# A graph layer with sorted gathers: loops written out, gathers paced by TensorE, row numbers copied once a block

## Chip, cores and metric

The kernel runs on one core of a Trainium2 chip. The metric is the time of one execution on the device in microseconds (us). TensorE multiplies matrices, VectorE and ScalarE work elementwise, GpSimd issues the gathers here, SyncE issues the plain transfers.

## What is computed

x has 50000 nodes of 128 features. 25000 edges carry 128 features each and name a node `src`; the sum of a node's edges is joined to the node's normalised features.

```python
h = jnp.maximum(_layernorm(x, axis=-1), 0.0)
agg = jax.ops.segment_sum(edge_attr, src, num_segments=50000)
z = jnp.concatenate([h, agg], axis=-1)            # 256 wide
z = jax.nn.silu(z @ W1 + b1)                      # W1 256 x 256
z = z @ W2 + b2                                   # W2 256 x 128
z = layernorm(z) * ln_gamma + ln_beta
out = x + (z + h)
```

## The kernel before

The work has two phases. In the **column phase** the 25000 edge numbers lie in 196 columns of 128. For each column VectorE makes one-hot matrices (`hot_tile`, `hot_slot`), TensorE counts with them (L601, L608) and fills a table (L613), and ScalarE reads ranks (L513, `rank_of`); three columns of 28 are VectorE's. At its end VectorE has turned the table into `slot_edge`: for each of 392 tiles of nodes, which edge stands in which of 128 slots (`slot_tables`, the first three blocks' part first).

In the **block phase** the nodes are taken in NB = 49 blocks of 1024 (8 tiles of 128, in two halves c = 0, 1 of four). GpSimd gathers each tile's edge rows from memory into `G[b % 3]` by an indirect DMA (L471). The row numbers are a column of `gather_rows`, which GpSimd copies from `slot_edge` just before (L459, `name_row`). The order of a gather's steps is: wait until `agg_done` says that block b-3 has left the buffer, copy the next tile's row numbers, wait for `row_named`, issue. Nothing else holds a gather back.

TensorE's `step(b)` is, for c = 0 and then 1: transpose four tiles of h (`turn_h`, L636: in c = 0 the second half of b, in c = 1 the first half of b+1), sum the gathered edges of that half by one-hots (`sum_edges`, L643, waits for `gathered`), layer 1 of half c (`layer1`, L654 to L659, two column groups m = 0, 1, each ends with `pre_done`), and layer 2 of the half before (`layer2`, L667 and L671, ends with `y_done`). ScalarE normalises x (L534), copies the high parts of `za` to `hi` (L541, L543), applies silu (L549) and squares y (L556). VectorE subtracts to get the low parts (L911, `split_low`, the first thing in its step), builds the one-hots HOT (L902), adds x and beta (L894), h (L919), takes statistics and reciprocal roots (`powers`), and scales the result (L927, L937). SyncE loads X four blocks ahead and stores R two blocks behind. The order on each engine is written out by hand; semaphores join the engines.

Both phases are loops. `run_columns` writes 28 columns out, then loops over turns of 28. `run_blocks` writes out the first `head` blocks (2 on ScalarE and SyncE, 3 on TensorE and GpSimd, 5 on VectorE), then loops over turns of 6 blocks, and writes out what is left, for TensorE blocks 39 to 48. In a loop, semaphore values and addresses are registers (`Turn`), and each wait on a register is an instruction of its own. A second copy of the whole gather code, from the table `spill`, runs instead when a tile has more edges than slots; it does not here, and stands ahead of the main copy. The loops' branches are at L285 (blocks) and L296 (columns).

## Time and profile before

| what | value |
|---|---|
| median of 3 runs | 835.01 us (830.93 to 836.53) |
| the profiled execution, its own time | 833.45 us |
| its span, first to last instruction | 831.8 us |
| busy share: TensorE, VectorE, GpSimd, ScalarE | 88%, 88%, 74%, 70% |
| mean granted TensorE clock | 0.957 |
| mean transfer rate | 79 GB/s |

The profiled time is the span and 1.65 us around it. A busy share is an average over both phases. The column phase ends near 125 us, where GpSimd begins its first copy of row numbers; everything after it is the block phase. A wait in the profile is named by what ended it; "issue" means that the profile shows no event that the engine waited for, and "remote" that it knows no instruction for the event.

### The profile page before, as it was taken

To read this page: it belongs to the slowest core of one execution; us is meant where nothing else is said; L and a number is where in the kernel's file an instruction comes from. 1 tells how busy PE (TensorE), PEld (TensorE's weight loads), DVE (VectorE), ACT (ScalarE), POOL (GpSimd) and SP (SyncE) were. 2 spreads that over 40 slices of the span, in tenths; PEclk is the share of its full clock that TensorE was granted. 3 is DMA by queue.
4 is the path that set the end of the run, shared out by engine and by line. 5 is a ranking of instruction groups with operands and counts; after the bars stand their busy time and mean duration, and the time that the engine had idled before them with its cause. 6 is when DMAs were issued, how large, how long until landed. Compare 5 with 4: busy or idle time off the path is not lost.

```text
span 831.8 us, 19347 instructions
## 1 busy us (share of the span) xinstructions
PE 734.6 (88%) x4567; PEld 602.0 (72%) x4616; DVE 734.0 (88%) x2494; ACT 585.6 (70%) x1927; POOL 617.9 (74%) x831
## 2 busy tenths in 40 slices
PE   4999973899899678998999899989988998989990
PEld 2455542788787657887888788878877887878880
DVE  6999994799996748998999899989888999997995
ACT  4999972687675636787687777868567877776861
POOL 4500006899888887999999989999898899898920
PEclk9999995999999988999999999999999999999996
DMA  5000000123232222332323223232323233231211
GB/s 185 2 0 0 0 0 18 47 71 111 84 122 73 71 73 69 120 121 70 119 76 115 94 93 121 87 103 93 98 73 118 83 107 122 72 102 60 69 58 46
DMA packets 28138, 65.49 MB, mean 79 GB/s; under 512 B 8379, under 2 KB 9934, under 8 KB 28070
## 3 DMA queue, kind: packets, MB, share of 16 engines
q1 hardware_dynamic: 15526, 51.90, 17.5%
q0 software_dynamic: 12544, 12.93, 6.9%
q14 instruction: 54, 0.44, 0.2%
q8 instruction: 14, 0.23, 0.1%
HBM read 51.98 MB, written 25.60 MB: 93 GB/s over the span
## 4 chain that ended last, share of the span: by engine, by line
POOL 35%; issue 26%; PE 25%; DVE 5%; ACT 3%; another core or an unknown queue 2%; DMA 2%; POOLq 1%; DVEq 0%; ACTq 0%; SPq 0%
POOL G L471 22%; POOL gather_rows L459 13%; PE y L671 4%; PE y L613 3%; PE za L643 3%; PE pre L654 2%; PE pre L655 2%; PE pre L659 2%; PE za L608 2%; PE pre L608 2%; PE pre L601 2%; PE za L636 1%; PE za L601 1%; DMA G<-in_edge_attr_dram,gather_rows 1%
## 5 line engine op out<-in xcount | busy, mean ns | idle before, releaser
L471 POOL DMA_INDIRECT G<-in_edge_attr_dram,gather_rows x392 | 450.1, 1148 | 69.1 <-POOL gather_rows L459 41.2
L459 POOL COPY gather_rows<-slot_edge 128x1 uint32 (+1 forms) x392 | 145.9, 372 | 98.4 <-DVE slot_edge L883 91.7
L671 PE MATMUL y<-w2c,S 128*128 128x128 f32 x1568 | 194.2, 276 | 6.5 <-issue 3.2
L671 PEld LDWEIGHTS y<-w2c,S 128*128 128x128 f32 x1568 | 192.9, 193 | 7.8 <-issue 5.3
L911 DVE TENSOR_TENSOR lo<-za,hi 128x1024 fp32r<-128x1024 f32 x98 | 119.7, 1221 | 72.5 <-ACT hi L543 37.8
L534 ACT ACTIVATE H<-X,shift,rstd 128x128 f32<-128x128 f32 x392 | 162.3, 505 | 22.7 <-DVE shift L793 22.7
L654 PE MATMUL pre<-hi,w1h 128*128 128x512 f32 x392 | 168.0, 429 | 0.7 <-issue 0.7
L655 PE MATMUL pre<-hi,w1l 128*128 128x512 f32 x392 | 158.8, 405 | 0.3
L541 ACT CAST hi<-za 128x512 fp32r<-128x512 f32 x98 | 57.5, 587 | 118.0 <-remote 55.0
L549 ACT ACTIVATE S<-pre,b1c 128x512 f32<-128x512 f32 x196 | 125.7, 693 | 9.2 <-remote 4.9
L659 PE MATMUL pre<-lo,w1h 128*128 128x512 f32 x392 | 125.9, 402 | 0.7 <-issue 0.7
L643 PE MATMUL za<-HOT,G 128*128 128x128 f32 x784 | 110.5, 286 | 17.8 <-DMA G<-in_edge_attr_dram,gather_rows 16.6
L643 PEld LDWEIGHTS za<-HOT,G 128*128 128x128 f32 x784 | 100.1, 200 | 20.8 <-DMA G<-in_edge_attr_dram,gather_rows 19.3
L738 DVE BATCH_NORM_STATS2 stat<-X 128x6 f32<-128x128 f32 x392 | 108.6, 283 | 0.0
L556 ACT ACTIVATE junk_sq<-y 128x128 bf16<-128x128 f32 x392 | 103.5, 287 | 3.5 <-PE y L671 3.5
L927 DVE SCALAR_TENSOR_TENSOR T<-y,rstd,gammas 128x128 f32<-128x128 f32 x392 | 105.6, 341 | 0.0
L543 ACT CAST hi<-za 128x512 fp32r<-128x512 f32 x98 | 57.6, 588 | 58.6 <-PE za L643 41.8
L636 PE MATMUL za<-ident,H 128*128 128x128 f32 x392 | 61.7, 281 | 37.3 <-ACT H L534 17.5
L659 PEld LDWEIGHTS pre<-lo,w1h 128*128 128x128 f32 x392 | 75.5, 193 | 19.3 <-issue 0.8
L654 PEld LDWEIGHTS pre<-hi,w1h 128*128 128x128 f32 x392 | 77.3, 197 | 15.0 <-issue 0.9
L655 PEld LDWEIGHTS pre<-hi,w1l 128*128 128x128 f32 x392 | 76.9, 196 | 15.4 <-issue 1.4
L556 ACT ACTIVATION_READ_ACCUMULATOR junk_sq<-y 128x1 f32 x392 | 85.5, 218 | 0.0
(123 smaller groups left out, 1042.2 us busy)
## 6 DMA issues: line engine op xcount, KB each, us to landing
X<-in_x_dram SPq DMA_DIRECT2D x48, 512.0 KB
out_dram<-R SPq DMA_DIRECT2D x48, 512.0 KB
G<-in_edge_attr_dram,gather_rows POOLq DMA_INDIRECT x392
X<-in_x_dram SPq DMA_DIRECT2D x1, 424.0 KB
out_dram<-R SPq DMA_DIRECT2D x2, 212.0 KB
w1f<-in_L_gnn_W_dram SPq DMA_DIRECT2D x1, 256.0 KB, 3.5
w2f<-in_L_gnn_W_dram SPq DMA_DIRECT2D x1, 128.0 KB, 2.7
srci<-in_src_dram SPq DMA_DIRECT2D x1, 97.2 KB
```

The costliest lines, as they stand in the source:

```text
L459: nc.gpsimd.tensor_copy(gather_rows[b.xj][:, t:t + 1], slot_edge[:, bass.ds(b.number(TILES, t), 1)]).then_inc(row_named, 1)
L471: nc.gpsimd.indirect_dma_start(G[b.j][:, t, :], None, source, bass.IndirectOffsetOnAxis(ap=gather_rows[b.xj][:, t:t + 1], axis=0), bounds_ ...
L534: done = nc.scalar.activation(H0[b.j][:, t, :], X[b.xj][:, t, :], ACT.Relu, bias=shift[b.j][:, t:t + 1], scale=rstd[b.j][:, t:t + 1])
L549: nc.scalar.activation(S[c][:, m, :], pre[m][:], ACT.Silu, bias=b1c[:, m:m + 1]).then_inc(silu_done, 1)
L556: done = nc.scalar.activation(junk_sq[:, p, c * HALF + t, :], y[2 * p + c][:, t * D:(t + 1) * D], ACT.Square, scale=float(D) ** -0.5, accu ...
L643: done = nc.tensor.matmul(za[:, 1, t * P:(t + 1) * P], G[b.j][:, c * HALF + t, :], HOT[b.j][:, c * HALF + t, :], start=True, stop=True)
L654: nc.tensor.matmul(pre[m][:], w1h[:, k, cols], hi[c][:, k, :], start=(k == 0), stop=False)
L655: nc.tensor.matmul(pre[m][:], w1l[:, k, cols], hi[c][:, k, :], start=False, stop=False)
L659: done = nc.tensor.matmul(pre[m][:], w1h[:, k, cols], lo[c][:, k, :], start=False, stop=(k == 1))
L671: done = nc.tensor.matmul(place[:, t * D:(t + 1) * D], S[c][:, m, t * P:(t + 1) * P], w2c[:, m, :], start=False, stop=(t == HALF - 1 and m ...
L738: done = nc.vector.bn_stats(stats[b.ring(2)][:, t, :], X[b.xj][:, t, :])
L911: nc.vector.tensor_tensor(out=lo[c][:], in0=za[:], in1=hi[c][:].bitcast(F32), op=ALU.subtract).then_inc(lo_done, 1)
```

## The change

All loops over columns and blocks are written out, so that semaphore values and addresses are constants. GpSimd copies the eight row numbers of a block in one instruction (`name_rows`), half a block ahead. A gather's wait for the freed buffer is replaced by a wait for an event on TensorE (`pace`): the four gathers of half c of block b+2 wait for the sum of edges in half-step c of TensorE's step b, for the two `pre_done` of that half-step's layer 1, and for its layer 2. The first two blocks are not paced. The spill copy of the gather code stands behind the main one.

```diff
-TURN_BLOCKS = 6
...
-        def run_blocks(engine, step, head=HEAD):
-
-            turns = (NB - 1 - head - X_AHEAD) // TURN_BLOCKS
-            for n in range(head):
+        def run_blocks(step):
+
+            for n in range(NB):
                 step(Block(n))
-            with engine.Fori(0, turns) as i:
-                turn = Turn(engine, i)
-                for n in range(head, head + TURN_BLOCKS):
-                    step(Block(n, TURN_BLOCKS, turn))
-            for n in range(head + turns * TURN_BLOCKS, NB):
-                step(Block(n))
-
-        def run_columns(engine, step, lag):
-
-            for n in range(UNROLL):
-                step(Item(n))
-            with engine.Fori(0, TURNS - 1) as i:
-                turn = Turn(engine, i)
-                for n in range(UNROLL, 2 * UNROLL):
-                    step(Item(n, UNROLL, turn))
-            for n in range(EC, EC + lag):
+
+        def run_columns(step, lag):
+
+            for n in range(EC + lag):
                 step(Item(n))
...
-            def name_row(b, t):
-
-                if t == 0:
-                    at_least(pool, agg_done, b.half(0, 1, 2 - 2 * X_RING), apart=pool_passed)
-                    if b.is_number(FIRST_BLOCKS):
-                        pool.wait_ge(slots_ready, 2)
-                nc.gpsimd.tensor_copy(gather_rows[b.xj][:, t:t + 1],
-                                      slot_edge[:, bass.ds(b.number(TILES, t), 1)]).then_inc(row_named, 1)
-
-            def gather(b, c, source, limit):
-
-                at_least(pool, agg_done, b.half(0, 1, 2 - 2 * RING), apart=pool_passed)
+            def name_rows(b):
+
+                at_least(pool, agg_done, b.half(0, 1, 2 - 2 * X_RING))
+                if b.is_number(FIRST_BLOCKS):
+                    pool.wait_ge(slots_ready, 2)
+                nc.gpsimd.tensor_copy(gather_rows[b.xj][:],
+                                      slot_edge[:, bass.ds(b.number(TILES), TILES)]).then_inc(rows_named, 1)
+
+            def pace(b, c, k):
+
+                if k == 0:
+                    at_least(pool, agg_done, b.half(1, 1, c + 1))
+                elif k == 3:
+                    at_least(pool, y_done, b.half(c, 1))
+                else:
+                    at_least(pool, pre_done, b.half(c, 2, k))
+
+            def gather(b, c, source, limit, pacer=None):
+
                 for t in range(c * HALF, (c + 1) * HALF):
-                    if t + 1 < TILES:
-                        name_row(b, t + 1)
-                    elif b.plus(1).exists(NB):
-                        name_row(b.plus(1), 0)
-                    at_least(pool, row_named, b.number(TILES, t + 1), apart=pool_passed)
+                    if t == HALF and b.plus(1).exists(NB):
+                        name_rows(b.plus(1))
+                    if t == 0:
+                        at_least(pool, rows_named, b.number(1, 1))
+                    if pacer is not None:
+                        pace(pacer, c, t - c * HALF)
                     nc.gpsimd.indirect_dma_start(
...
-                            gather(b.plus(2), c, source, limit)
-
-                run_blocks(pool, step, head=3)
+                            gather(b.plus(2), c, source, limit, pacer=b)
+
+                run_blocks(step)
...
-            name_row(Block(0), 0)
+            name_rows(Block(0))
+            with pool.If(flag == 0):
+                gather_all(edge_attr, edges - 1)
             with pool.If(flag != 0):
                 gather_all(spill, NB * BLOCK - 1)
-            with pool.If(flag == 0):
-                gather_all(edge_attr, edges - 1)
```

On GpSimd, before, this is the entry of the block loop in the main copy of the gathers, from the first branch on; `row_named` counts the copies, and an ISA row is a register or semaphore instruction.

```order
L285 UNCONDITIONAL_BRANCH
L285 ISA
L459 ISA [waits agg_done]
L459 COPY gather_rows<-slot_edge 128x1
L471 DMA G<-in_edge_attr_dram,gather_rows 128x128 [waits row_named]
L459 ISA
L459 COPY gather_rows<-slot_edge 128x1
L471 DMA G<-in_edge_attr_dram,gather_rows 128x128 [waits row_named]
L459 ISA
```

On GpSimd, after, this is one block and the head of the next in the middle of the block phase; L417 is the copy and L438 the gather.

```order
L438 DMA G<-in_edge_attr_dram,gather_rows 128x128 [waits agg_done,rows_named]
L438 DMA G<-in_edge_attr_dram,gather_rows 128x128 [waits pre_done] x2
L438 DMA G<-in_edge_attr_dram,gather_rows 128x128 [waits y_done]
L417 COPY gather_rows<-slot_edge 128x8 [waits agg_done]
L438 DMA G<-in_edge_attr_dram,gather_rows 128x128 [waits agg_done]
L438 DMA G<-in_edge_attr_dram,gather_rows 128x128 [waits pre_done] x2
L438 DMA G<-in_edge_attr_dram,gather_rows 128x128 [waits y_done]
```

Eight pairs of copy and gather have become one copy and eight gathers, and every gather has a wait on TensorE that it did not have.

On VectorE, before, this is the end of the block loop's body, its branch, and what follows the loop; L911 is the first instruction of a step, so that it stands at the head of the body too.

```order
L919 TENSOR_TENSOR R<-H,R 128x512 [waits h0_done,xb_done]
L764 REGISTER_ALU
L791 SCALAR_TENSOR_TENSOR rstd<-guess_off,guess 128x16 [waits small]
L764 REGISTER_ALU
L793 SCALAR_TENSOR_TENSOR shift<-msum,rstd 128x8 [waits small]
L285 REGISTER_ALU
L285 COMPARE_AND_BRANCH
L911 TENSOR_TENSOR lo<-za,hi 128x1024 [waits pre_done,hi_done]
L902 TENSOR_TENSOR HOT<-iota_node,slot_node 128x512 [waits agg_done]
```

On VectorE, after, this is the same place between two steps (L886 was L919, L878 was L911).

```order
L886 TENSOR_TENSOR R<-H,R 128x512 [waits h0_done,xb_done]
L758 SCALAR_TENSOR_TENSOR rstd<-guess_off,guess 128x16 [waits small]
L760 SCALAR_TENSOR_TENSOR shift<-msum,rstd 128x8 [waits small]
L878 TENSOR_TENSOR lo<-za,hi 128x1024 [waits pre_done,hi_done]
L869 TENSOR_TENSOR HOT<-iota_node,slot_node 128x512 [waits agg_done]
```

The branch and the register instructions are gone; the order of the others is the same.

## Rows read from the trace of the kernel before

**Rows 1.** The page: TensorE and VectorE busy, and the chain by engine.

```profile
PE 734.6 (88%) x4567; PEld 602.0 (72%) x4616; DVE 734.0 (88%) x2494; ACT 585.6 (70%) x1927; POOL 617.9 (74%) x831
...
POOL 35%; issue 26%; PE 25%; DVE 5%; ACT 3%; another core or an unknown queue 2%; DMA 2%; POOLq 1%; DVEq 0%; ACTq 0%; SPq 0%
```

**Rows 2.** Timeline of TensorE at S(0), S(8), S(13), S(15), S(32), S(39), S(48): start, duration.

```profile
141.65 0.66 PE L636 MATMUL za<-ident,H 128*128 128x128 f32 x2 [2.02 <-DVE lo L911]
...
247.93 0.49 PE L636 MATMUL za<-ident,H 128*128 128x128 f32 x3
...
335.87 0.60 PE L636 MATMUL za<-ident,H 128*128 128x128 f32 x4
...
360.46 0.60 PE L636 MATMUL za<-ident,H 128*128 128x128 f32 x4
...
582.98 0.38 PE L636 MATMUL za<-ident,H 128*128 128x128 f32 x2
...
678.99 0.49 PE L636 MATMUL za<-ident,H 128*128 128x128 f32 x3
...
799.92 0.49 PE L636 MATMUL za<-ident,H 128*128 128x128 f32 x3
```

**Rows 3.** Windows: stretch and length, busy per engine (count), clock, DMA share, GB/s.

```profile
247.93:335.87 87.94, 70.63 (x407) 59.51 (x411) 62.06 (x214) 48.69 (x160) 75.07 (x105) 0.90 0.27 84
...
354.80:379.40 24.60, 24.46 (x165) 21.57 (x166) 24.50 (x86) 19.41 (x65) 22.29 (x29) 1.00 0.32 104
```

**Rows 4.** GpSimd's two groups on the page, and timeline rows beside VectorE's.

```profile
L471 POOL DMA_INDIRECT G<-in_edge_attr_dram,gather_rows x392 | 450.1, 1148 | 69.1 <-POOL gather_rows L459 41.2
L459 POOL COPY gather_rows<-slot_edge 128x1 uint32 (+1 forms) x392 | 145.9, 372 | 98.4 <-DVE slot_edge L883 91.7
...
134.95 1.03 POOL L471 DMA_INDIRECT G<-in_edge_attr_dram,gather_rows  x1 [0.16 <-POOL gather_rows L459]
...
157.58 0.68 DVE L894 TENSOR_TENSOR R<-X,betas 128x512 f32<-128x512 f32 x1
157.64 0.68 POOL L459 COPY gather_rows<-slot_edge 128x1 uint32<-128x1 uint32 x1
...
158.48 1.39 POOL L471 DMA_INDIRECT G<-in_edge_attr_dram,gather_rows  x1 [0.16 <-issue]
```

**Rows 5.** Waits from 678 to 800, then block 44's last gather and its sum.

```profile
PE za L643 <- DMA G<-in_edge_attr_dram,gather_rows: 6.1, 2, 4.1
...
742.00 1.30 POOL L471 DMA_INDIRECT G<-in_edge_attr_dram,gather_rows  x1 [0.16 <-POOL gather_rows L459]
...
742.79 0.28 SPq L332 DMA_DIRECT2D X<-in_x_dram  x1
...
749.51 1.86 PE L643 MATMUL za<-HOT,G 128*128 128x128 f32 x8 [4.09 <-DMA G<-in_edge_attr_dram,gather_rows]
```

**Rows 6.** Timeline at one of the turns of VectorE's loop.

```profile
392.44 1.23 DVE L911 TENSOR_TENSOR lo<-za,hi 128x1024 fp32r<-128x1024 f32 x1 [2.94 <-issue]
...
393.81 0.63 PE L636 MATMUL za<-ident,H 128*128 128x128 f32 x4 [2.45 <-DVE lo L911]
```

**Rows 7.** Waits (total, times, longest): ScalarE and TensorE 247 to 336, ScalarE 582 to 679.

```profile
ACT hi L541 <- remote: 26.8, 5, 9.5
...
PE y L671 <- issue: 3.2, 9, 0.5
...
ACT hi L541 <- remote: 12.1, 5, 4.3
```

**Rows 8.** Window in the column phase, columns as in rows 3.

```profile
59.00:74.00 15.00, 14.79 (x88) 8.23 (x87) 14.43 (x43) 14.72 (x53) 0.00 (x0) 1.00 0.00 0
```

**Rows 9.** Timeline of the first gathers, and TensorE's first sum.

```profile
128.12 0.20 POOL L459 COPY gather_rows<-slot_edge 128x1 uint32<-128x1 uint32 x1 [2.19 <-issue]
...
130.57 1.25 POOL L471 DMA_INDIRECT G<-in_edge_attr_dram,gather_rows  x1 [2.25 <-issue]
...
137.55 0.58 PE L643 MATMUL za<-HOT,G 128*128 128x128 f32 x1 [5.18 <-DMA G<-in_edge_attr_dram,gather_rows]
```

65 lines of the change are left out of this document (23 added, 42 removed).

## The prediction

> **What bounds the kernel now.** I read the page first, then the windows, then the timeline of TensorE, and last the timelines of the engines that TensorE waits for. The page says that TensorE and VectorE are each busy 88% of the span and that the chain that ended last gives most of its length to GpSimd and to "issue" [rows 1]. So no engine is simply full; one has to ask block by block who is late.
>
> The ruler for that is the first transpose of the second half of a block (L636), which opens block b's step on TensorE. Call its start S(b). S(0) is 141.65, S(8) 247.93, S(13) 335.87, S(15) 360.46, S(32) 582.98, S(39) 678.99, S(48) 799.92 [rows 2]. From S(13) to S(15) it takes 24.59 us for two blocks, 12.29 us a block. In that stretch TensorE is busy 24.46 of 24.60 us and VectorE 24.50, with a granted clock of 1.00, the level of 2.4 GHz [rows 3]: TensorE is full, VectorE nearly so, and GpSimd has 2.3 us to spare. Thus 12.29 us is the floor of a block for this arithmetic. 48 blocks at the floor are 590 us; S(48)-S(0) is 658.3, so **68.4 us are lost** in the block phase. By stretch, time less 12.29 a block: blocks 0 to 8: 106.3 - 98.3 = 8.0; 8 to 13: 87.9 - 61.5 = 26.5; 13 to 32: 247.1 - 233.5 = 13.6; 32 to 39: 96.0 - 86.0 = 10.0; 39 to 48: 120.9 - 110.6 = 10.3.
>
> Who takes them? A gather on GpSimd alone takes 1.03 us [rows 4], but their mean is 1.148 and that of the copy before each is 0.372, since VectorE's two-input instructions hold them up: beside x plus beta (L894) a copy took 0.68 and a gather 1.39 [rows 4]. With the 0.16 us between copy and gather a tile costs 1.148 + 0.372 + 0.16 = 1.68 us, a block 13.4 us: **more than the floor**. GpSimd never waits for another engine to speak of; it issues gathers without a pause and loses about 1.1 us a block on TensorE until TensorE waits for it, unless something else has held TensorE up before. Two of the stretches (0 to 8, 39 to 48) are of this kind: in the last, TensorE waits 6.1 us for gathered rows in two waits of up to 4.1, with what follows each [rows 5]. The stretch 13 to 32 is another kind. Three times VectorE's first instruction after its loop's branch (L911) starts some 3 us late with "issue" as the reason, and TensorE's next transposes wait on it: 2.94 and then 2.45 us at 392 to 394 [rows 6]; three such turns make most of the 13.6 us, 4.2 apiece with what is lost around them. The stretch 8 to 13 has one such turn and 22 us more whose cause I can't read: ScalarE waits 26.8 us in five waits for something "remote" (the trace names no releaser), and TensorE's granted clock was 0.90 in the mean, part of it at the lower level of 1.2 GHz [rows 3]. Blocks 32 to 39 have the same sign, 12.1 us of it [rows 7].
>
> **The change part by part.**
> (1) *One copy of row numbers per block.* GpSimd loses seven copies, 7 x 0.372 = 2.6 us a block; the 0.16 ahead of each gather I keep. What is left is 8 x (1.148 + 0.16) plus one copy of eight columns. No row shows that copy; the one-column copy runs 0.37 in the mean and 0.68 where it is held up, and twice that bounds it above, so 0.2 to 1.4, and I take 0.4, as eight numbers a partition are still few. 10.5 + 0.4 = 10.9 us a block, under 12.29 by 1.4 (by the bounds 1.6 to 0.4). GpSimd stops being the late one. Worth: 8.0 + 10.3 us in the stretches it rules, and its part of blocks 32 to 39.
> (2) *No block loops.* The three turns in 13 to 32 go, most of 13.6 us; one turn in 8 to 13 goes (4.2) and one in 32 to 39 (4). Registers that carried semaphore values go too; TensorE has no idle time for these in the floor stretch, so I cost them at nothing, hidden under matmuls.
> The Trainium skill (Runtime: NRT & Kernel Launch, Instruction fetch mechanics) says that each engine fetches its instructions in order ahead of use and that a taken branch out of the fetched pages stalls until the target is fetched; by that rule, the late L911 right behind VectorE's branch is a fetch, and it vanishes in straight code. The sum above goes by the rows alone.
> (3) *No column loops.* Before the blocks ScalarE is busy 14.72 of 15 us at ranks [rows 8], instruction behind instruction. A loop's branch leaves no idle time to recover: nothing, at most 2 us.
> (4) *The spill branch behind the main one, and the start.* GpSimd loses 2.19 and 2.25 us to "issue" around the first gathers, and TensorE waits 5.18 us for the first gathered rows [rows 9]. The second pause follows the branch that jumps over a whole copy of the gather code, which now stands behind. Bounds 0 to 4.4 us, plus 0.6 for the three copies that no longer stand between the first four gathers (3 x 0.35 = 1.1 us, less what the larger first copy takes). I take 3 us.
> (5) *The added waits.* Gather t of a half of block b+2 now waits for agg_done, pre_done twice and y_done of TensorE's half-step of block b. Behind a waiting gather GpSimd has only later gathers and the next block's copy queued. The last gather of a half is freed when that half-step ends and its rows are wanted two half-steps after that, by sum_edges one whole block later: 12.29 us, less 1.39 for the gather itself, 10.9 us to land. What landing takes: the first rows came 1.6 us after their fourth gather's end [rows 4, 9], and the longest that I found is block 44's, whose last gather ends at 743.30 and whose sum starts at 749.51, 6.2 us [rows 5], just as SyncE had issued a block's load. So 4.7 us remain in the worst row: I cost the waits at nothing. They are hidden by that slack; if it were gone, each us of excess would cost 1 us a block.
>
> **Sum.** Saved without dispute: 8.0 + 10.3 + 13.6 + 4.2 + 4 = 40.1, and 3 at the start: 43.1. In dispute: the 22.3 us left in blocks 8 to 13 and 6 us in 32 to 39, 28.3 together. That they are of the loops speaks that both lie inside them while the straight stretch 39 to 48 has nothing of the kind beside its gather waits; against it speaks that blocks 13 to 32 lie in loops too and are clean. I let two thirds go, 19. I keep 2 us lost in the first blocks, where VectorE also makes the slot tables. 43.1 + 19 - 2 = 60 us. The span becomes 831.8 - 60 = 772, the profiled time 833.45 - 60 = 773.5; the median of the runs (835.01) lies 1.6 above the profiled one, so **775 us**.
> Bounds: all 68.4 gone, 4.4 at the start and 2 in the columns make 75 us: 760. None of the disputed 28.3 and nothing at the start give 43.1 - 3 - 2 = 38 us: 797.
>
> **Rivals.**
> *The disputed stalls stay* (they are no loop's and no gather's): 794 to 797, worked out just now. Chance 0.17.
> *The floor falls too.* Seven fewer reads by GpSimd might speed VectorE, and all stalls go: 760 or less. But TensorE is full at 12.29, so VectorE's gain buys nothing. 0.07.
> *GpSimd meets VectorE more often.* Paced by TensorE, each gather falls on the same VectorE instruction in every block. If all eight were beside two-input ones, as the 1.39 row, a block would be 8 x (1.39 + 0.16) + 0.8 = 13.2 us, 0.9 over the floor, 48 x 0.9 = 44 us more: 818. Against: those instructions fill under half of VectorE's time and come in different half-steps. 0.04. The Trainium skill (SBUF — State Buffer, SBUF: two separate sides) states the rule behind it, that the port pair shared by GpSimd and VectorE is an exclusive lock that whoever comes first holds for the whole instruction; the 1.39 against 1.02 agrees.
> *Slower: straight code starves an engine.* Each turn's stall was 4.2 us, with "issue" and no event as its reason, as where instructions aren't at hand. The unrolled code has some two and a half times as many different instructions on TensorE. If that fails at one place in every block, 48 x 4.2 = 202 us are added; it outweighs the saving from 15 stalls on, one in three blocks. For it: in blocks 8 to 13 TensorE waited nine times with "issue" before layer-2 matmuls [rows 7]. Against it: blocks 39 to 48 are straight code on every engine and hold the floor in between two gather waits. 0.03, at about 850 or more.
> *The pacing doesn't pace, or delays nothing* is no case of its own: the time is as forecast.
>
> **How the numbers follow.** Forecast (two stretches freed, turns gone, part of the disputed gone; 760 to 790): 0.69. Range 760 to 797: it takes in forecast and the first rival, 0.86, less the edges. A measurement of this kernel can tell about 1% from no change. Faster by over 1%: 0.69 + 0.17 + 0.07 + 0.04 = 0.97, less 0.01 for the spread of the last (818); within 1%: 0.01; slower: 0.03.
>
> **What would show it.** Right: GpSimd's idle time before gathers is released by TensorE's sums and matmuls, S(b) advances by 12.29 us in nearly every block, no L911 starts 3 us late behind a branch, and no wait of TensorE for G is over 1 us after block 1. GpSimd's mean gather stays near 1.15. Wrong: TensorE waits for G again (port or landing), "issue" before TensorE or VectorE once in some blocks (delivery of instructions), or a block that takes over 12.6 us with TensorE full, which would say that my floor isn't one.

## The result and the profile after

The changed kernel takes 811.33 us in the median of four runs (809.54 to 812.34), the kernel before 834.88 beside it (830.93 to 836.53): a ratio of 0.972 [0.968, 0.976]. It is faster, by 23.5 us. The forecast was 775 us, in a range of 760 to 797. The sign is right, and less than half of the gain is there. The profiled run took 809.54 us with a span of 808.0. Here and below a median is of all runs, while a ratio and its interval leave out runs over 1.5% above the fastest of their kernel.

First, the page of the changed kernel: the engines, the chain by engine, and the groups that matter. L603 is the transposes (L636 before), L610 the sum of edges (L643), L508 and L510 ScalarE's two high copies (L541 and L543), L878 VectorE's low copy (L911), L438 the gather.

```profile
PE 723.1 (89%) x4567; PEld 591.0 (73%) x4616; DVE 730.6 (90%) x2494; ACT 581.6 (72%) x1927; POOL 502.9 (62%) x488
...
PE 63%; ACT 17%; DVE 8%; issue 7%; another core or an unknown queue 3%; DMA 1%; SPq 0%; POOL 0%; DVEq 0%; ACTq 0%; POOLq 0%
...
L438 POOL DMA_INDIRECT G<-in_edge_attr_dram,gather_rows x392 | 470.7, 1201 | 162.4 <-issue 105.7
...
L878 DVE TENSOR_TENSOR lo<-za,hi 128x1024 fp32r<-128x1024 f32 x98 | 119.7, 1222 | 51.3 <-ACT hi L510 47.1
...
L508 ACT CAST hi<-za 128x512 fp32r<-128x512 f32 x98 | 58.2, 594 | 90.8 <-PE za L603 63.5
L510 ACT CAST hi<-za 128x512 fp32r<-128x512 f32 x98 | 57.6, 587 | 79.5 <-remote 63.3
...
L610 PE MATMUL za<-HOT,G 128*128 128x128 f32 x784 | 105.5, 278 | 2.4 <-DMA G<-in_edge_attr_dram,gather_rows 2.4
...
L603 PE MATMUL za<-ident,H 128*128 128x128 f32 x392 | 62.7, 283 | 41.1 <-issue 23.9
```

Against [rows 1], GpSimd has left the chain (35% to 0%) and fell from 74 to 62% busy. TensorE waits for gathered rows 2.4 us in all. That is what the change is for, and it works. But TensorE now waits 41.1 us at its transposes, and ScalarE 79.5 us before its second high copy, mostly for "remote".

With the prediction's ruler, S(b):

```profile
137.29 1.09 PE L603 MATMUL za<-ident,H 128*128 128x128 f32 x4 [2.02 <-DVE lo L878]
...
158.09 0.60 PE L603 MATMUL za<-ident,H 128*128 128x128 f32 x4
...
776.21 0.60 PE L603 MATMUL za<-ident,H 128*128 128x128 f32 x4
```

S(0) is 137.29 (141.65 before, [rows 2]), S(1) 158.09, S(48) 776.21. The start gave 4.4 us. The block phase fell from 658.3 to 638.9 us, so that 638.9 - 48 x 12.29 = 49.0 us are lost where 68.4 were: 8.5 in the first block and 40.5 in the next 47, 0.86 a block. What follows S(48) is as long as before (31.8 and 31.9 us). So 4.4 + 19.4 = 23.8 us, the whole difference of the spans.

The loss has another shape now. Before, a block took 12.29 us for long stretches and some 16.4 at a turn of a loop. Now 31 of the 47 blocks after the first take 13.2 to 13.6 us, and the others 12.3 to 13.0. By the prediction's stretches, the time above 12.29 us a block was 8.0, 26.5, 13.6, 10.0 and 10.3 us before (blocks 0 to 8, 8 to 13, 13 to 32, 32 to 39, 39 to 48), and is 12.3 (8.5 of it in the first block), 5.6, 16.5, 7.5 and 7.2 us now. The windows of the changed kernel show a block of each kind (columns as in [rows 3]):

```profile
170.36:182.66 12.30, 12.23 (x84) 10.79 (x84) 12.27 (x44) 10.55 (x34) 8.77 (x9) 1.00 0.26 85
...
591.72:605.10 13.38, 12.45 (x84) 10.82 (x83) 12.37 (x44) 9.69 (x33) 10.19 (x10) 1.00 0.32 104
```

The same work, the same clock (1.00, the level of 2.4 GHz), and in the second 0.9 us in which TensorE stands. The timeline of the block from 591.72 shows how it comes about (TensorE first, then ScalarE, VectorE, and TensorE again):

```profile
591.72 0.60 PE L603 MATMUL za<-ident,H 128*128 128x128 f32 x4
592.16 1.06 PE L610 MATMUL za<-HOT,G 128*128 128x128 f32 x8
...
593.47 0.59 ACT L508 CAST hi<-za 128x512 fp32r<-128x512 f32 x1 [1.69 <-PE za L603]
595.69 0.58 ACT L510 CAST hi<-za 128x512 fp32r<-128x512 f32 x1 [1.64 <-remote]
...
597.18 1.66 ACT L501 ACTIVATE H<-X,shift,rstd 128x128 f32<-128x128 f32 x4
...
596.31 1.22 DVE L878 TENSOR_TENSOR lo<-za,hi 128x1024 fp32r<-128x1024 f32 x1 [0.98 <-ACT hi L510]
...
598.89 0.66 PE L603 MATMUL za<-ident,H 128*128 128x128 f32 x4 [0.86 <-issue]
```

The transposes are recorded as done at 592.32 and the sum at 593.22. ScalarE waits for each by a semaphore and starts its copies at 593.47 and 595.69, 1.15 and 2.47 us after. What ScalarE does next moves with them: the normalised tiles of the next block are ready at 598.84, and TensorE wants them 0.86 us sooner. I call this a **late signal**. The times of the semaphore events in the trace agree: that of the sum comes 2.5 us after the recorded end, while from 200 to 710 us none of VectorE's and ScalarE's own events lags by more than 0.01. The ends of matmuls are modelled, so it may be the matmuls' results that are late and not the signal. Either way the receiver gets it then.

The traces have a second sign. In that same stretch the changed kernel's trace holds only 71% of the semaphore events that the instructions of TensorE, VectorE and ScalarE must have caused. Every trace in this document with late signals holds 67 to 74% of them, and every trace without holds 98 to 100%. What loses the records isn't known.

### The profile page after: what moved, and what is told of

Read it like the earlier page. It is cut to its first block, busy times and chain, and to the rows that moved or that the text cites. A ratio compares the mean times of both kernels' runs of the same rounds, so it can differ in the third digit from the quotient of the medians.

```text
span 808.0 us, 15586 instructions
## 1 busy us (share of the span) xinstructions
PE 723.1 (89%) x4567; PEld 591.0 (73%) x4616; DVE 730.6 (90%) x2494; ACT 581.6 (72%) x1927; POOL 502.9 (62%) x488
## 4 chain that ended last, share of the span: by engine, by line
PE 63%; ACT 17%; DVE 8%; issue 7%; another core or an unknown queue 3%; DMA 1%; SPq 0%; POOL 0%; DVEq 0%; ACTq 0%; POOLq 0%
PE y L638 18%; ACT junk_rank L480 10%; PE pre L626 9%; PE pre L621 9%; PE pre L622 9%; PE za L610 9%; PE za L603 7%; ACT H L501 3%; ACT junk_sq L523 2%; DVE T L894 1%; PE y L634 1%; ACT hi L508 1%; DVE hot_tile L776 1%; DMA srci<-in_src_dram 1%
## 5 line engine op out<-in xcount | busy, mean ns | idle before, releaser
L438 POOL DMA_INDIRECT G<-in_edge_attr_dram,gather_rows x392 | 470.7, 1201 | 162.4 <-issue 105.7
L638 PE MATMUL y<-w2c,S 128*128 128x128 f32 x1568 | 191.6, 276 | 3.5 <-issue 0.2
L621 PE MATMUL pre<-hi,w1h 128*128 128x512 f32 x392 | 164.3, 419 | 5.0 <-ACT S L516 5.0
L878 DVE TENSOR_TENSOR lo<-za,hi 128x1024 fp32r<-128x1024 f32 x98 | 119.7, 1222 | 51.3 <-ACT hi L510 47.1
L622 PE MATMUL pre<-hi,w1l 128*128 128x512 f32 x392 | 155.9, 398 | 0.0
L626 PE MATMUL pre<-lo,w1h 128*128 128x512 f32 x392 | 124.1, 397 | 0.0
L508 ACT CAST hi<-za 128x512 fp32r<-128x512 f32 x98 | 58.2, 594 | 90.8 <-PE za L603 63.5
L510 ACT CAST hi<-za 128x512 fp32r<-128x512 f32 x98 | 57.6, 587 | 79.5 <-remote 63.3
L610 PE MATMUL za<-HOT,G 128*128 128x128 f32 x784 | 105.5, 278 | 2.4 <-DMA G<-in_edge_attr_dram,gather_rows 2.4
L894 DVE SCALAR_TENSOR_TENSOR T<-y,rstd,gammas 128x128 f32<-128x128 f32 x392 | 105.7, 341 | 0.0
L603 PE MATMUL za<-ident,H 128*128 128x128 f32 x392 | 62.7, 283 | 41.1 <-issue 23.9
L610 PEld LDWEIGHTS za<-HOT,G 128*128 128x128 f32 x784 | 96.9, 195 | 2.8 <-DMA G<-in_edge_attr_dram,gather_rows 2.8
L621 PEld LDWEIGHTS pre<-hi,w1h 128*128 128x128 f32 x392 | 74.6, 190 | 19.1 <-issue 3.2
L622 PEld LDWEIGHTS pre<-hi,w1l 128*128 128x128 f32 x392 | 74.7, 190 | 13.3
L603 PEld LDWEIGHTS za<-ident,H 128*128 128x128 f32 x392 | 43.9, 142 | 51.0 <-issue 42.1
```

Source lines behind the costliest of these rows:

```text
L438: nc.gpsimd.indirect_dma_start(G[b.j][:, t, :], None, source, bass.IndirectOffsetOnAxis(ap=gather_rows[b.xj][:, t:t + 1], axis=0), bounds_ ...
L603: done = nc.tensor.transpose(za[:, 0, t * P:(t + 1) * P], H0[b.j][:, c * HALF + t, :], ident[:])
L610: done = nc.tensor.matmul(za[:, 1, t * P:(t + 1) * P], G[b.j][:, c * HALF + t, :], HOT[b.j][:, c * HALF + t, :], start=True, stop=True)
L621: nc.tensor.matmul(pre[m][:], w1h[:, k, cols], hi[c][:, k, :], start=(k == 0), stop=False)
L622: nc.tensor.matmul(pre[m][:], w1l[:, k, cols], hi[c][:, k, :], start=False, stop=False)
L626: done = nc.tensor.matmul(pre[m][:], w1h[:, k, cols], lo[c][:, k, :], start=False, stop=(k == 1))
```

## The experiments

In the diffs, minus is the changed kernel and plus the experiment, unless another is named; they show the lines that matter. Every kernel except the two with "loops" in its name is written out as the changed kernel is. The kernels of a group ran on one chip, with the kernel before beside them, and I give its median, since it turned out to matter.

### Which part of the change does what

Four kernels on one chip (kernel before: 836.73 us).

**nopace**: the pacing waits go, the wait that protects the buffer returns.

```diff
+                at_least(pool, agg_done, b.half(0, 1, 2 - 2 * RING))
...
-                    if pacer is not None:
-                        pace(pacer, c, t - c * HALF)
```

> The changed kernel with the paced waits taken out: a half's gathers wait, as in the kernel before, only for block b-3 to have left the buffer; loops written out and one copy of row numbers a block stay. Theory P (the pacing costs: gathers tied to TensorE's steps bring about the 13.4 us a block of the changed kernel): blocks go back to 12.3 us, 765 to 780 us. Theory U (straight code costs, whatever GpSimd does): 13.4 us a block stays, 805 to 815 us.

**unroll_only**: no pacing, and eight copies a block again, one ahead of each gather.

```diff
-                nc.gpsimd.tensor_copy(gather_rows[b.xj][:],
-                                      slot_edge[:, bass.ds(b.number(TILES), TILES)]).then_inc(rows_named, 1)
+                nc.gpsimd.tensor_copy(gather_rows[b.xj][:, t:t + 1],
+                                      slot_edge[:, bass.ds(b.number(TILES, t), 1)]).then_inc(rows_named, 1)
...
+                at_least(pool, agg_done, b.half(0, 1, 2 - 2 * RING))
...
-                    if pacer is not None:
-                        pace(pacer, c, t - c * HALF)
```

> The changed kernel with GpSimd as before: eight one-column copies a block, no pacing; only the loops are written out. Theory P: GpSimd's 13.4 to 13.7 us a block decide, no stalls at loop turns, 800 to 810 us. Theory U: GpSimd's pace and the loss in straight code together, 810 to 825 us, S(b) advances by over 13.4 us.

**loops_onecopy**: the kernel before with its loops, and one copy of eight columns a block.

```diff
--- the kernel before
+++ loops_onecopy
-                nc.gpsimd.tensor_copy(gather_rows[b.xj][:, t:t + 1],
-                                      slot_edge[:, bass.ds(b.number(TILES, t), 1)]).then_inc(row_named, 1)
+                nc.gpsimd.tensor_copy(gather_rows[b.xj][:],
+                                      slot_edge[:, bass.ds(b.number(TILES), TILES)]).then_inc(row_named, 1)
```

> The kernel before with one copy of row numbers a block and nothing else changed: loops kept, no pacing. Theory P: 12.3 us a block but for the loop turns (three to five of 4.2 us) and the unexplained stalls of blocks 8 to 13: 790 to 815 us. Theory U: the same blocks in loops at 12.3 us, those written out (0 to 2, 39 to 48) at 13.4.

**loops_paced**: the same with the pacing waits in the place of the wait for the freed buffer. The diff is against loops_onecopy.

```diff
+                    if pacer is not None:
+                        pace(pacer, c, t - c * HALF)
```

> The kernel before with one copy a block and with the pacing of the changed kernel, loops kept. Theory P: 13.4 us a block also inside the loops, and the loop turns on top, 820 to 835 us. Theory U: 12.3 us inside the loops, as without pacing, 790 to 815 us.

Measured: nopace 809.51 us, ratio 0.971 [0.961, 0.981]; unroll_only 811.79, 0.968 [0.958, 0.978]; loops_onecopy 842.18, 1.008 [1.004, 1.011]; loops_paced 832.98, 0.999 [0.994, 1.003]. **Writing the code out gives the whole gain by itself on this chip; the single copy gives nothing without it and nothing measurable beside it; pacing neither costs nor gives beside written-out code**, and with loops it is worth 1%. unroll_only has the spill branch in its new place too, so that the 4.9 us which it gains at S(0) (136.77 us, 141.65 before) are of both. Both theories that these runs were to tell apart, that pacing eats the gain and that straight code does, fall.

But equal times come from unequal traces. unroll_only loses 33.8 - 12.3 us in the second block, so GpSimd gets 27 us ahead of the sums. Then blocks take 12.29 us up to block 10 while that lead shrinks, as here (TensorE's transposes in the two halves of each block, 6.15 us apart):

```profile
223.36 0.60 PE L595 MATMUL za<-ident,H 128*128 128x128 f32 x4
229.51 0.60 PE L595 MATMUL za<-ident,H 128*128 128x128 f32 x4
235.65 0.60 PE L595 MATMUL za<-ident,H 128*128 128x128 f32 x4
241.80 0.60 PE L595 MATMUL za<-ident,H 128*128 128x128 f32 x4
```

From block 19 on the lead is 1.5 us, and a block takes 13.1 us, GpSimd's own pace with eight copies:

```profile
L430 POOL DMA_INDIRECT G<-in_edge_attr_dram,gather_rows x392 | 445.6, 1137 | 63.2 <-POOL gather_rows L418 45.8 <-issue 17.4
L418 POOL COPY gather_rows<-slot_edge 128x1 uint32<-128x1 uint32 x392 | 137.6, 351 | 97.1 <-DVE slot_edge L842 89.5 <-PE za L602 4.7 <-remote 0.4
```

8 x (1.137 + 0.351 + 0.16) = 13.2. nopace has one copy a block and no late gather (its leads are 24 us), yet a block takes 12.85 us with late signals. The changed kernel's takes 13.4, and loops_onecopy's 12.3 to 13.8 with 16.3 or 16.4 at each turn. The copies that were saved are given back as late signals.

### Is it GpSimd's copies, its waits, or the gathers?

Four kernels on a second chip (kernel before: 834.93 us).

**paced_8copies**: unroll_only with the pacing waits. The diff is against unroll_only.

```diff
+                    if pacer is not None:
+                        pace(pacer, c, t - c * HALF)
```

> The changed kernel, with eight small copies a block on GpSimd again, one ahead of each gather, and the pacing kept. Theory T (TensorE's signals come late whenever GpSimd sits waiting for TensorE's semaphores): the block stays at about 13.4 us, since the waits are the same, and the time is 809 to 815 us. Rival D (gathers that follow one another 1.3 us apart load the DMA path, and a copy between them spreads them): the block falls towards the 12.29 us that the written-out kernel with eight copies and no pacing had in its blocks 5 to 14, and the time goes to 770 to 790 us.

**wait_scalar**: the pacing waits for ScalarE's events.

```diff
                 if k == 0:
-                    at_least(pool, agg_done, b.half(1, 1, c + 1))
-                elif k == 3:
-                    at_least(pool, y_done, b.half(c, 1))
+                    at_least(pool, hi_done, b.half(1, 1, c + 1))
+                elif k == 1:
+                    at_least(pool, h0_done, b.half(c, 1, 3))
                 else:
-                    at_least(pool, pre_done, b.half(c, 2, k))
+                    at_least(pool, silu_done, b.half(c, 2, k - 1))
```

> The changed kernel, but each of the four waits of a half is for an event of ScalarE (its high copy, its normalised tiles, its two SiLUs) instead of TensorE's sums, layer 1 and layer 2. Theory T: nobody but ScalarE and VectorE listens to TensorE, its signals come on time again, the block goes to about 12.3 us, the time to 765 to 780 us. Rival D: nothing changes, 13.4 us a block and 808 to 815 us.

**one_wait**: of the four waits only that of k = 0.

```diff
-                elif k == 3:
-                    at_least(pool, y_done, b.half(c, 1))
-                else:
-                    at_least(pool, pre_done, b.half(c, 2, k))
```

> The changed kernel with one pacing wait a half (for the sum of the next half) instead of four, so that the four gathers of a half follow one another without a wait. Theory T: fewer waits on TensorE's events, the block takes 12.5 to 13.0 us and the time is 785 to 805 us. Rival D: denser gathers, the block takes 13.4 to 13.8 us and the time is 811 to 830 us. If neither matters, 808 to 815 us.

**no_gather**: the step's gathers and copies end after block 3, and TensorE doesn't wait for any after that. It leaves out the sum of edges of the later blocks.

```diff
-                    if t == HALF and b.plus(1).exists(NB):
+                    if t == HALF and b.plus(1).exists(4):
...
-                    if b.plus(2).exists(NB):
+                    if b.plus(2).exists(4):
...
-                pe.wait_ge(gathered[b.j][c], b.lap(16 * HALF, 16 * HALF))
+                if b.exists(4):
+                    pe.wait_ge(gathered[b.j][c], b.lap(16 * HALF, 16 * HALF))
```

> The changed kernel without GpSimd's copies and gathers from block 4 on; TensorE then sums what the three buffers still hold, without waiting. It leaves out that part of the computation. Theories T and D both say that the three other engines alone turn at 12.29 us a block from block 4 on, some 755 to 770 us in all. Rival C (the straight code or the three engines' own handovers cost it, and the gathers have nothing to do with it): the block stays at about 13.4 us and the time at 805 to 812 us.

Measured: paced_8copies 805.48 us, 0.965 [0.956, 0.973]; wait_scalar 821.99, 0.987 [0.979, 0.994]; one_wait 811.85, 0.966 [0.954, 0.978]; no_gather 768.33, 0.922 [0.915, 0.929].

no_gather is the clear one: S(b) advances by 12.29 us in every block from 4 to 48. **The floor of the prediction is real, on the same chip on which the other three have late signals, and only with the gathers is the block lifted off it.** The handovers of the three engines and the straight code by themselves are not at fault, and rival C falls. The kernel takes away three things at once, GpSimd's copies, its gathers and the gathered data, so it can't say which of them matters. The waits of 200 to 710 in no_gather:

```profile
ACT hi L508 <- PE za L603: 73.0, 81, 1.0
ACT hi L510 <- PE za L611: 25.5, 83, 0.3
```

No wait for "remote", none over 1.0 us. Beside it, wait_scalar from 184 to 774:

```profile
ACT hi L508 <- remote: 101.3, 37, 3.0
POOL G L438 <- ACT H L501: 51.7, 36, 1.5
```

GpSimd's pacing listens to ScalarE alone here (what is left is one wait a block for the sum of edges six blocks before the one whose rows are copied, long met), and TensorE's signals are as late as ever, 13.5 us a block. Theory T, by which GpSimd's waits for TensorE's semaphores make them late, is wrong. The profiled run of one_wait (814.60 us, of runs from 800.21 to 815.52) takes 12.88 us a block up to block 13 and then 13.41, with 15.1 in blocks 13, 25 and 37: two steady rhythms in one program. The two fastest of its runs may differ. paced_8copies sits at 13.1 to 13.2 us a block with a lead of 1.5, again bound by eight copies.

### Spacing, bytes, and the chip

I then supposed that back-to-back gathers hold TensorE's signals, and that a gap or a copy between them lets the signals through. Four kernels on a third chip (kernel before: 819.82 us).

**four_copies**: no pacing; four copies a block, each of two gathers' row numbers.

```diff
+                nc.gpsimd.tensor_copy(gather_rows[b.xj][:, t:t + 2],
+                                      slot_edge[:, bass.ds(b.number(TILES, t), 2)]).then_inc(rows_named, 1)
...
+                    if t % 2 == 0:
+                        if t + 2 < TILES:
+                            name_row(b, t + 2)
+                        elif b.plus(1).exists(NB):
+                            name_row(b.plus(1), 0)
+                        at_least(pool, rows_named, b.number(TILES // 2, t // 2 + 1))
```

> The written-out kernel without pacing, with four copies a block, each of the row numbers of two gathers, so that GpSimd stops for a copy and its signal after every second gather. Theory H (TensorE's signals are held back while GpSimd starts gather after gather with 0.30 us between them, and get through when it stops for a copy; eight copies cost GpSimd 13.1 us a block, one copy costs signals): GpSimd needs some 12 us a block, the signals come at most 1 us late, the block takes 12.3 to 12.7 us and the time is 780 to 800 us. Rival E (any two gathers without a copy between them do the harm): 12.9 to 13.4 us a block and 805 to 815 us.

**idle_gap**: nopace with waits that are always met. The diff is against nopace.

```diff
+                    for _ in range(4):
+                        pool.wait_ge(late_const, 1)
                     nc.gpsimd.indirect_dma_start(
```

> The written-out kernel without pacing and with one copy a block, with four waits that are always met ahead of each gather, so that GpSimd's queue has some instructions more between two gathers and no more work on memory. Theory H with a pause alone (time between gathers is what lets the signals through): the block falls to 12.3 to 12.7 us and the time to 780 to 800 us. Rival K (it is the copy, or the wait for its signal, that lets them through): 12.85 us a block as without these waits, 805 to 815 us.

**quarter_bytes**: nopace, with smaller pieces; it leaves out three quarters of the edge features. The diff is against nopace.

```diff
-                        G[b.j][:, t, :], None, source,
+                        G[b.j][:, t, 0:D // 4], None, source[:, :].rearrange("n (a b) -> (n a) b", a=4),
```

> The written-out kernel without pacing and with one copy a block; each gather fetches 128 pieces of 128 bytes where it fetched 128 rows of 512 bytes, so that only a quarter of the edge features is summed: it leaves out the rest. GpSimd starts as many gathers of as many descriptors, the DMA engines move a quarter of the bytes. Theory H: no change, 12.85 us a block and 805 to 815 us. Rival D (the gathers' data on its way through the DMA engines is what delays the handovers): the block falls to 12.3 to 12.5 us and the time to 775 to 790 us.

**sync_loads**: no_gather, with plain loads from SyncE's queue in the gathers' place, for which TensorE waits; it leaves out the choice of the rows. The diff is against no_gather.

```diff
+                    for c in range(2):
+                        sp.dma_start(G[b.j][:, c * HALF:(c + 1) * HALF, :], edge_attr[0:P * HALF, :]
+                                     .rearrange("(p t) d -> p t d", t=HALF)).then_inc(filled[b.j][c], 16)
```

> The changed kernel without GpSimd's gathers from block 4 on; the buffers are filled instead by two plain loads a block of the same bytes from SyncE's queue, always the first 512 rows: it leaves out the choice of the rows. Theory H: TensorE's signals are on time, 12.29 us a block as without gathers, 765 to 775 us. Rival D: the same bytes go the same way into the same buffers, so 12.8 to 13.4 us a block and 795 to 815 us.

Measured: four_copies 769.33 us, 0.939 [0.936, 0.941]; idle_gap 763.38, 0.932 [0.929, 0.935]; quarter_bytes 766.72, 0.934 [0.930, 0.938]; sync_loads 761.21, 0.929 [0.926, 0.930].

That read like a success of all four ideas at once, which made me distrust it: no late signal in any of the four, though idle_gap's gathers follow one another 0.30 us apart exactly as nopace's do, so its four waits add nothing to the gap (GpSimd's queue passes them while the gather before is still at work). Either these kernels differ from the earlier ones, or this chip does. So nopace, four_copies, unroll_only and the changed kernel went together to one more chip, and idle_gap to another. Each of the next passages was written before its run; the runs are after_again, nopace_again, four_copies_again, unroll_again and idle_gap_again, in this order.

> The changed kernel once more, now on the same chip as the unpaced, the eight-copy and the four-copy kernel. Theory X (the late signals belong to some chips and not to others): on a chip where the kernel before takes about 820 us it has no late signals, 12.3 to 12.5 us a block and 765 to 780 us; on one where that takes about 835 us it repeats 13.4 us a block and 811 us. Theory H (they belong to the kernels): 13.4 us a block and a ratio of 0.972 on either.

> The written-out kernel with one copy a block and no pacing once more. Theory X: 760 to 775 us where before takes 820 us, 810 us where that takes 835 us. Theory H: a ratio of 0.971 and 12.85 us a block on either, and clearly slower than the kernel with four idle waits before each gather (0.932).

> The written-out kernel with four copies a block and no pacing once more. Theory X: on a chip where before takes 835 us it has late signals too, 12.8 to 13.2 us a block and 800 to 812 us; where that takes 820 us, 769 us. Theory H: no late signals and a ratio of 0.939 on either.

> The written-out kernel with eight copies a block and no pacing once more. GpSimd needs 13.1 us a block with eight copies on any chip. Theory X: where before takes 820 us the start loses nothing, so that 48 blocks of 13.1 us give 795 to 805 us, slower than all with fewer copies; where that takes 835 us, 811 us and no difference. Theory H: 0.968 on either, level with the others.

> The kernel with four idle waits before each gather once more. Theory X (the late signals belong to some chips): where the kernel before takes about 835 us it has late signals, about 12.85 us a block and 805 to 818 us, as the same kernel without the idle waits; where that takes 820 us, 763 us again. Theory K (the idle waits keep the signals on time): no late signal and a ratio of 0.93 on either.

Measured on the fourth chip (kernel before: 837.08 us): after_again 811.45 us, 0.975 [0.969, 0.981]; nopace_again 813.81, 0.968 [0.959, 0.978]; four_copies_again 817.60, 0.982 [0.975, 0.988]; unroll_again 807.07, 0.969 [0.963, 0.974]. On the fifth (kernel before: 824.80): idle_gap_again 804.59, 0.975 [0.970, 0.979].

**The same kernel, four_copies, is 0.939 on one chip and 0.982 on another; idle_gap 0.932 and 0.975.** The intervals are far apart, while no line of the kernels changed. Each chip was used on one occasion only, so what differs may be the chip or the occasion; I say chip for short. The rule that I expected to tell the chips apart by, before at 820 or at 835 us, is not exact, since on the fifth chip the kernel before took 824.8 and signals were late all the same. The two traces of idle_gap show the difference. First the waits of 200 to 710 on the third chip, then of the same stretch on the fifth:

```profile
POOL G L439 <- issue: 94.7, 330, 0.3
ACT hi L509 <- PE za L604: 77.2, 82, 0.9
ACT hi L511 <- PE za L611: 32.6, 82, 2.0
...
DVE lo L879 <- ACT hi L511: 4.7, 11, 1.1
PE za L611 <- DMA G<-in_edge_attr_dram,gather_rows: 3.3, 7, 1.4
```

```profile
ACT hi L509 <- remote: 49.4, 29, 2.5
ACT hi L509 <- PE za L604: 24.1, 32, 2.0
...
POOL G L439 <- PE za L611: 21.3, 19, 1.2
ACT hi L511 <- PE za L611: 17.9, 26, 1.5
ACT hi L511 <- remote: 16.1, 17, 1.6
...
PE za L604 <- ACT H L502: 6.5, 15, 0.9
```

On the third chip not one wait is for "remote" and TensorE never waits at its transposes; on the fifth both come back. There the start goes wrong as well (TensorE's timeline, and then one of the waits from 136.38 to 187.22):

```profile
136.38 1.09 PE L604 MATMUL za<-ident,H 128*128 128x128 f32 x4 [2.03 <-DVE lo L879]
...
163.76 0.37 PE L639 MATMUL y<-w2c,S 128*128 128x128 f32 x1 [1.72 <-issue]
...
172.96 1.11 PE L604 MATMUL za<-ident,H 128*128 128x128 f32 x4 [4.63 <-ACT H L502]
...
ACT hi L511 <- remote: 12.7, 1, 12.7
```

The kernel before has the same picture once, in the disputed stretch, from S(11) on (TensorE's timeline, and then waits from 282 to 330; the longest one of ScalarE ends at 306.16):

```profile
304.68 0.36 PE L671 MATMUL y<-w2c,S 128*128 128x128 f32 x1 [0.46 <-issue]
...
ACT hi L541 <- remote: 18.2, 3, 9.5
...
PE za L636 <- ACT H L534: 3.9, 1, 3.9
```

I call this a **pause**: layer 2's matmuls stand apart with "issue" between them, ScalarE waits 9.5 or 12.7 us for one event of TensorE, and the block takes 25.6 us (before) or 36.6 (here). Twelve of the fourteen traces with late signals have a block of 19 us or more with an event of TensorE 7.3 us late or later, all but that of the kernel before in the first two blocks (20.8 us for the changed kernel's first), and so has no_gather while it still gathers. None of the third and sixth chip has: no block takes over 13.9 us there. From 297.00 to 313.60 in the kernel before TensorE is busy 9.59 of 16.60 us with a granted clock of 0.77 in the mean, and in the 6.4 us after it the clock is 0.52, nearly all at the lower level of 1.2 GHz.

S(1) - S(0) is 36.6 us on the fifth chip, against 12.38 on the third chip. In that pause GpSimd runs 27 us ahead, and from then on it must wait for TensorE at most buffers; on the third chip it keeps a lead of 3.2 to 5.2 us from block 2 to block 43 and waits for nobody. So idle_gap has two ways to run: no pause, a small lead, signals on time; or a pause, a large lead, late signals. The three don't always go together: unroll_only had the pause and the lead and then ten blocks with signals on time, and unroll_again had no pause at its start and took 17.6 us from S(12) to S(13), with signals up to 5.7 us late. Nor is waiting for TensorE the cause: in nopace_again the blocks in which GpSimd didn't wait have late signals too, and so have many blocks of the kernel before, where it never waits in the middle stretches.

Last, quarter_bytes again, to part bytes from gathers on a chip with late signals:

> The kernel whose gathers bring 128 pieces of 128 bytes instead of 128 rows of 512 bytes, once more; it leaves out three quarters of the edge features. On a chip with late signals: theory H' (the gathers themselves, GpSimd's work and their descriptors, delay them): late signals as before, 12.8 to 13.0 us a block and a ratio of 0.965 to 0.98. Rival D (the bytes do): no late signal, 12.3 to 12.5 us a block and a ratio of 0.925 to 0.94. On a chip without them it tells nothing new: 0.934.

Measured on a sixth chip (kernel before: 820.63 us): 765.23 us, 0.934 [0.930, 0.937], 12.29 us in most blocks, no late signal. It repeats the result of the third chip, but since no kernel with full gathers ran on this one, it doesn't tell whether the bytes or the chip did it. The same holds for sync_loads: it ran only on the third chip, where full gathers have no late signals either.

## Why the prediction was wrong

**The floor: right.** 12.29 us a block is what the three engines need: 45 blocks in a row in no_gather, and long rows of them elsewhere. My own sign against it, a block over 12.6 us with TensorE full, didn't appear; TensorE is busy 12.45 of 13.38 us.

**GpSimd's pace (part 1): mis-sized, and not where the error lies.** I put 10.9 us on a block: 8 x (1.148 + 0.16) + 0.4. The group rows of idle_gap on the third chip, where GpSimd waits for nobody after the start, and then the one place in the kernel before where two gathers follow one another without a copy:

```profile
L439 POOL DMA_INDIRECT G<-in_edge_attr_dram,gather_rows x392 | 475.6, 1213 | 113.9 <-issue 113.9
L417 POOL COPY gather_rows<-slot_edge 128x8 uint32<-128x8 uint32 x49 | 15.4, 315 | 89.8 <-DVE slot_edge L851 89.6
```

```profile
793.98 1.03 POOL L471 DMA_INDIRECT G<-in_edge_attr_dram,gather_rows  x1 [0.15 <-issue]
795.31 1.82 POOL L471 DMA_INDIRECT G<-in_edge_attr_dram,gather_rows  x1 [0.30 <-issue]
```

8 x (1.213 + 0.291) + 0.315 = 12.35 us. The gap between two gathers isn't the 0.16 of [rows 4], which stood between a copy and a gather, but 0.30, and the trace of the kernel before had it at 795.31. So one copy a block brings GpSimd from 13.2 to 12.35, just level with TensorE, and not 1.4 below it. The copy's guess (0.4) was good. The gather of 1.39 us in [rows 4] was read beside the wrong instruction: L894 had ended at 158.26, before it began at 158.48, and it lay beside L919 (158.27 to 158.95), which has two inputs as well.

**The loops' turns (part 2): right in the mechanism.** In the written-out code no L878 waits over 0.8 us with "issue", where L911 waited 2.94 behind its branch [rows 6]. In loops_onecopy a block with a turn still took 16.3 or 16.4 us, 4 above the floor. The Trainium skill (Runtime: NRT & Kernel Launch, Instruction fetch mechanics) says that a taken branch to a page that hasn't been fetched stalls the engine; the 2.94 us and their absence in straight code agree with it. But the time that the turns gave back was lost again in the same blocks, see below.

**The column loops and the start (parts 3 and 4): right.** VectorE's first part of `slot_edge` ends at 123.63 us where it ended at 125.16, so the columns gave 1.5 us (I had 0 to 2), and the start after it the other 2.8 of the 4.4 at S(0) (I had 3).

**The waits (part 5): right as far as they can be measured.** The changed kernel and the one without waits are at 0.975 and 0.968 on one chip, with intervals that overlap. Landings were not late: the changed kernel's TensorE waits 2.4 us for G in all.

**The step that failed: freed blocks were put at the floor.** The sum took 57 us out of the block phase (60 less 3 at the start), so that 11.4 of the 68.4 would be left; 49.0 are. The prediction asked only whether stalls that it had seen would go, and let every block without one fall to 12.29 us. That TensorE's signals could come late in blocks which had not shown it stood in no term; it was put at nothing. **The runs show 0.86 us a block in its place**, 40.5 us in 47 blocks, and 8.5 us of a pause in the first. By stretch: in blocks 13 to 32, where 13.6 us were counted as saved without dispute, 16.5 are lost now; in 39 to 48, where 10.3 were, 7.2 are lost; in 32 to 39 it is 7.5 of 10.0. The changed kernel's second run on the fourth chip repeats this (19.0, 6.9, 7.0).

**The dispute was decided on a wrong ground, and is not where the error lies.** I let two thirds of 28.3 us of stalls go with the loops, since they lay inside loops. They aren't the loops': written-out kernels have both late signals and pauses, and no_gather, with the same straight code, has neither after block 3. The largest of those stalls was a pause (the 9.51 us above). Yet in blocks 8 to 13 only 5.6 of 26.5 us are left, about what the two thirds leave (22.3 / 3 = 7.4). That is luck: pauses fall at different places in different kernels, loops_onecopy with all its loops has none in these blocks, and the changed kernel has one in its first block. Had all the disputed stalls stayed, the sum would still have given 797, not 811. So my first rival ("the disputed stalls stay", 794 to 797) was right that they are no loop's, wrong that they are no gather's, and took them for a fixed sum. I had named the argument for it, that blocks 13 to 32 lie in loops too and are clean: a stall that some stretches of the same looped code have and others don't isn't the loop's.

On the third chip the forecast's gain is there for a kernel close to the changed one: idle_gap took 763.38 us and the kernel before 819.82, 56 us less and a ratio of 0.932, where 775 to 835 is 0.928; 8.7 us are lost in its block phase. Whether the changed kernel itself gains as much there wasn't tried.

**The other rivals.** The port rival forecast one figure near the truth (818) for another reason: its sign would have been a longer block by GpSimd and waits for G, and there are none (2.4 us). The sign of starved straight code, "issue" before TensorE, did appear: 23.9 us before L603. But in the block shown above those tiles were ready at 598.84 and the transposes began at 598.89, so they waited for data; and no_gather, the same straight code, runs at the floor.

**What stays open.** What makes TensorE's signals late. Shown: it takes GpSimd's gathers or what comes with them (none in no_gather after block 3), and it differs from chip to chip with the same kernel. Not shown: whether it is GpSimd's work or the gathered data, since quarter_bytes and sync_loads ran only where nothing was late; why a pause comes (the "issue" waits of TensorE in it look like waiting for instructions, but that was only read and not tried); whether the recording of events plays a part, since the traces with late signals are those with lost records and no time on record is known to be of an unrecorded run; and whether GpSimd's lead, the phase of its gathers, or the chip itself keeps the late state going.

## What to carry to other kernels

Don't put freed blocks at the floor because some blocks reach it: ask what else was seen anywhere in the trace (here events that came late for no reason given) and price it in every block, above all when the change removes what now hides it. A stall whose cause can't be read goes into the rival at its full size, and may grow. Price a back-to-back sequence by the gap of two neighbours of the same kind, not by the gap of the pair that is being taken apart. And before believing an experiment that brought everything expected, run it once more beside its control on the same chip: here idle_gap turned from 0.932 to 0.975 and four_copies from 0.939 to 0.982.

## What the runs showed of the hardware

- A receiver can see TensorE's event 1 to 2.5 us after the recorded end of the matmul (2.47 in the block above), in a steady rhythm block after block, on four chips in most stretches in which GpSimd gathers. In no_gather, and in every kernel on the third and sixth chip, no event of TensorE came over 0.02 us after the recorded end from 200 to 710.
- A pause is something else than the rhythm: one block of 19 to 37 us, with ScalarE waiting up to 12.7 us for one event of TensorE and layer 2's matmuls standing apart meanwhile (idle_gap on the fifth chip, 157 to 171 us), only on the chips that have late signals.
- The same kernel took 763 us on one chip and 805 us on another, and 769 and 818, while the kernel before differed by 0.6 and 2.1% only: these ratios of a kernel to a baseline don't carry over between chips.
- The gap between two indirect gathers is 0.30 us, that between a copy and a gather 0.16; four waits already met between two gathers add nothing to it. A gather beside VectorE's instructions with two inputs in SBUF took 2.26 us against 1.00 alone. The timeline of idle_gap on the third chip, GpSimd and then VectorE:

```profile
502.81 1.01 POOL L439 DMA_INDIRECT G<-in_edge_attr_dram,gather_rows  x1 [0.30 <-issue]
504.12 1.00 POOL L439 DMA_INDIRECT G<-in_edge_attr_dram,gather_rows  x1 [0.30 <-issue]
505.43 2.26 POOL L439 DMA_INDIRECT G<-in_edge_attr_dram,gather_rows  x1 [0.30 <-issue]
507.99 1.00 POOL L439 DMA_INDIRECT G<-in_edge_attr_dram,gather_rows  x1 [0.30 <-issue]
...
504.93 1.28 DVE L905 TENSOR_TENSOR R<-T,R 128x512 f32<-128x512 f32 x2
506.13 0.68 DVE L887 TENSOR_TENSOR R<-H,R 128x512 f32<-128x512 f32 x1
506.75 1.23 DVE L879 TENSOR_TENSOR lo<-za,hi 128x1024 fp32r<-128x1024 f32 x1
```

  The gather that starts at 505.43 ends at 507.69. Of the three VectorE rows only L905 and L887 have both inputs in SBUF, and they end at 506.81, 0.88 us before the gather does; L879 reads `za` from PSUM, and the gather ended while it ran. The Trainium skill (SBUF — State Buffer, SBUF: two separate sides) says that GpSimd and VectorE share a port pair that one of them holds for a whole instruction, VectorE among others when it has two inputs in SBUF and GpSimd's instruction reads SBUF. A gather, which reads its row numbers there, that gets most of its 1.00 us only after the last such instruction agrees with it.
